# An adaLN model on one core: the steps of both attentions written out instead of looped

## The chip, the core and the metric

The kernel runs on one core of a Trainium2 chip. A core has five engines with an instruction stream each: TensorE (PE, with its weight loads shown as PEld), VectorE (DVE), ScalarE (ACT), GpSimd (POOL) and SyncE (SP), which here issues all DMAs. They meet only through semaphores: an instruction waits until a counter has reached a value, and raises one when it is done. The metric is the time of one execution on the device in microseconds.

## What is computed

Two transformer layers over x of 32 batches of 256 tokens with 128 features, each layer with an attention and a feed-forward part, both scaled and shifted per batch by a modulation table that is computed first. 16 heads of 8 features. Cut to what matters for the change:

```python
# layer 0, attention: no softmax
q, k = l2_normalize(x_norm @ w_q), l2_normalize(x_norm @ w_k)          # per head
resonance = 0.5 + 0.5 * tanh((q @ k.T - 0.27) * 15.0)
fused = (resonance * gate_q[:, None] * gate_k[None, :]) @ v            # gates: sigmoids of q.g_q, k.g_k
x = x + gate * (fused @ w_o + b_o)
# layer 0, feed-forward: 32 x 4 expert slots, tokens picked by the largest logit of their group
# layer 1, attention: rope on q and k, softmax
x = x + gate * (softmax(q @ k.T / sqrt(8)) @ v @ Wo + bo)
# layer 1, feed-forward: ternary weights, gelu-like gate
```

## The kernel before, in words

x stays in on-chip memory from the first step to the last. Four stages follow each other: attention 0 (`attention_0`, from about 30 to 400 us), the experts (`experts_0`, written out, to about 630), attention 1 (`attention_1_bounded`, to about 952; a general form, `attention_1`, is compiled too and chosen by a branch at run time, but isn't run with these inputs) and the feed-forward part (`ffn_1`, a loop of its own over 16 tiles).

Both attentions are software pipelines over the 32 batches. One step b holds, on every engine, work of several batches: TensorE computes the scores of batch b in eight chunks (`scores`), the weighted sums of heads (`heads`), the transposes of keys and queries of batch b+1 (`turn_keys`, `turn_queries`), the projections of b+2 and the transposes of b+3 (`turn`). ScalarE takes each score chunk through tanh (line 686) or exp (line 2439). VectorE normalises, splits q and k into two halves of 16 bits (`a_stack`), copies transposed keys and queries out of PSUM (`a_kT` line 841, `a_qT` line 846), runs a nine-step Newton iteration in attention 0 (`newton_step`, `a_norm2c` first), and adds the residual. GpSimd computes reciprocal roots (`a_rstd`, line 407), applies the modulation and doubles the queries. SyncE loads x and table rows some steps ahead.

The order on each engine is the order in which its `step(b, p)` calls these functions; p is the parity of b and picks one of two buffers. Engines wait with constants where b is a number and with a register's value where b is a loop variable. `stepped` decides which: it writes out the steps up to `pair_first`, then runs a loop of two steps a pass, then writes out the rest. Called as (-3, 33, 4, 12) for attention 0 and (-1, 33, 4, 12) for attention 1, it puts steps 4 to 27 into twelve passes; 0 to 3 and 28 to 31 are written out. In a looped step the address of a tile (`bass.ds(b * TT, TT)`) and the value of a wait (`b * CHUNKS + c`) are computed by register instructions of the engine's sequencer; they appear in the trace as ALU_OP and FUSED_REGOPS, and at the end of a pass there is a COMPARE_BRANCH (line 79). In layer 0 a step of VectorE begins, by the trace, with the copy `a_stack` of line 810, the last instruction of the step before; it is used below as the mark of the step.

Of the kernel before, what the change touches and what calls it, by code (L numbers as in the profile page):

```python
# [24 lines left out]
B = 32  # L25
# [35 lines left out]
def wait(eng, sem, n):  # L61

    if isinstance(n, int) and n <= 0:
        return
    eng.wait_ge(sem, n)
# [9 lines left out]
def stepped(eng, first, last, pair_first, pair_count, step):  # L75

    for b in range(first, pair_first):
        step(b, b % 2)
    with eng.Fori(0, pair_count) as i:
        step(i * 2 + pair_first, pair_first % 2)  # L80
        step(i * 2 + (pair_first + 1), (pair_first + 1) % 2)
    for b in range(pair_first + 2 * pair_count, last + 1):
        step(b, b % 2)
# [210 lines left out]
def attention_0(nc, ctx, dram, sbuf, psum, following):  # L294
# [75 lines left out]
    def rows_of(b, row, n):  # L370
        src = dram["table"]
        src = src[bass.ds(b, 1), row:row + n, :] if not isinstance(b, int) else src[b:b + 1, row:row + n, :]
        return src.rearrange("o r d -> (o r d)").partition_broadcast(P)
# [5 lines left out]
    def there(b):  # L379
        return not isinstance(b, int) or 0 <= b < B  # L380
# [2 lines left out]
        return min(n, B) if isinstance(n, int) else n  # L383

    def every(eng, step):
        stepped(eng, -3, B + 1, 4, 12, step)

    def load(sp, n, p):

        wait(sp, h_done, n - 1)  # L390
        wait(sp, mod_norm_loaded, n * 16)
        sp.dma_start(mod_norm[p][:, :, :], rows_of(n, ROW_CA0, 2)).then_inc(mod_norm_loaded, 16)

        if isinstance(n, int) and n < FIRST:
            return
        wait(sp, x_loaded, (n - FIRST) * 16)
        sp.dma_start(tiles(n), x_rows(n)).then_inc(x_loaded, 16)
# [90 lines left out]
    def run():  # L488
        with nc.Block() as block:
            @block.sync  # L490
            def _(sp):
                def load_gate(n, p):

                    wait(sp, x_biased, n - 1)
                    wait(sp, wo_done, n - 1)
                    sp.dma_start(mod_gate[p][:, :, :], rows_of(n, ROW_GA0, 2)).then_inc(mod_gate_loaded[p], 16)

                def step(b, p):
                    if there(b + 4):
                        load(sp, b + 4, p)  # L500
                    if there(b + 1):
                        load_gate(b + 1, 1 - p)

                load(sp, 1, 1)
                sp.wait_ge(dram["table_stored"], 32)
                load_gate(0, 0)
                load(sp, 2, 0)
                load(sp, 3, 1)

                for dst, src in dram["experts_loads"]:  # L510
                    sp.dma_start(dst, src).then_inc(dram["experts_loaded"], 16)
                for n in range(HB):
                    following["load"](sp, n)
                stepped(sp, 0, B - 1, 4, 12, step)

            @block.tensor
            def _(pe):
# [101 lines left out]
                def step(b, p):  # L619
                    if isinstance(b, int) and b == -2:  # L620
                        pe.wait_ge(wg_done, 2)
                    for pair in range(CHUNKS // 2):
# [23 lines left out]
                        if pair == 3:  # L646
                            if there(b - 1):
                                project_out(b - 1, 1 - p)
                            if there(b + 3) and not (isinstance(b, int) and b == -1):
                                turn(b + 3)  # L650

                every(pe, step)

            @block.scalar
            def _(act):
# [34 lines left out]
                def step(b, p):  # L690
                    for c in range(CHUNKS):
# [6 lines left out]
                        if c == 5 and there(b):  # L698
                            gT_out(b)

                every(act, step)

            @block.gpsimd
            def _(pool):
# [32 lines left out]
                nc.gpsimd.memset(ones16[:, :], 1.0).then_inc(ones_set, 1)  # L737
                pool.wait_ge(ones_set, 1)
                every(pool, step)

            @block.vector
# [1476 lines left out]
def attention_1_bounded(nc, ctx, dram, sbuf, psum, ffn_opening, opening):  # L2218
# [51 lines left out]
    def gate_rows(b):  # L2270
        src = dram["table"]
        src = (src[bass.ds(b, 1), ROW_GA1:ROW_GA1 + 2, :] if not isinstance(b, int)
               else src[b:b + 1, ROW_GA1:ROW_GA1 + 2, :])
        return src.rearrange("o r d -> (o r d)").partition_broadcast(P)

    def there(b):
        return not isinstance(b, int) or 0 <= b < B

    def every(eng, step):
        stepped(eng, -1, B + 1, 4, 12, step)  # L2280


    def sync(sp):
        def load_gate(n, p):

            wait(sp, x_biased, n - 1)
            wait(sp, wo_done, n - 1)
            sp.dma_start(mod_gate[p][:, :, :], gate_rows(n)).then_inc(mod_gate_loaded[p], 16)

        def step(b, p):  # L2290
            if there(b + 1):
                load_gate(b + 1, 1 - p)

        load_gate(0, 0)

        for dst, src in dram["ffn_loads"]:
            sp.dma_start(dst, src).then_inc(dram["ffn_loaded"], 16)
        stepped(sp, 0, B - 1, 4, 12, step)

    def tensor(pe):  # L2300
        def project_v(n, p):
# [79 lines left out]
        def step(b, p):  # L2381
            for pair in range(CHUNKS // 2):
# [24 lines left out]
                if pair == 3:  # L2407
# [9 lines left out]
                    elif b == B - 1:  # L2417
                        ffn_opening["turn"](pe, 1)

        every(pe, step)  # L2420

    def scalar(act):
# [30 lines left out]
    def gpsimd(pool):  # L2453
# [33 lines left out]

        padding(0)
        every(pool, step)

    def vector(dve):
# [98 lines left out]
        every(dve, step)  # L2590

    return {"sync": sync, "tensor": tensor, "scalar": scalar, "gpsimd": gpsimd, "vector": vector}


# [640 lines left out]
```

## Time and profile before

| | us |
|---|---|
| median of 3 runs | 1316.62 |
| lowest, highest | 1313.14, 1316.94 |
| span of the profiled execution | 1317.2 |

The profile is of one execution of the same program, with the start and end of every instruction on every engine. "Idle before" is the time in which an engine did nothing ahead of an instruction, and what follows the arrow is what ended it; "issue" means that nothing the profile shows was waited for. The instructions of a sequencer (waits, register operations, branches) don't count as busy. Half of the span belongs to stages that the change doesn't touch.

### The profile page before, as it was taken

The page shows a single profiled execution, that of the slowest core. Times are in us where ns is not written, and L with a number is a line of the kernel's source. Part 1 is how long each engine was busy: PE and PEld are TensorE (multiplying, and loading weights), DVE is VectorE, ACT ScalarE, POOL GpSimd, SP SyncE. Part 2 cuts the span into 40 slices and gives each one's busy share as a digit, 9 for nine tenths or more (in the row PEclk, how much of TensorE's full clock was granted, in tenths as well). Part 3 has the DMA queues.
Part 4 walks back from the last instruction along what each step waited for, and adds up shares of the span by engine and source line. Part 5 has one row for each costly group of instructions (what it writes and reads, how often), then busy time and mean ns, then how long its engine had stood idle before and what let it go on. Part 6 is the DMA issues. An engine that isn't in the chain of part 4 may idle for free.

```text
span 1317.2 us, 39867 instructions
## 1 busy us (share of the span) xinstructions
PE 1220.9 (93%) x13717; PEld 812.8 (62%) x13717; DVE 1054.6 (80%) x2935; ACT 932.2 (71%) x1338; POOL 574.3 (44%) x793
## 2 busy tenths in 40 slices
PE   3899999999997899987899999999879999999998
PEld 2555555555544666766555555555458877878776
DVE  5799999999976787756899999999646777777763
ACT  0698888888894565542688888888747676766665
POOL 2454444454431243323333343343236565655653
PEclk7799999999999999998899999999979999999999
DMA  5411111111001222100300000000000000000000
GB/s 140 143 33 33 34 36 36 36 36 36 28 10 47 53 50 62 48 19 2 105 14 16 12 12 16 12 12 17 6 2 9 9 16 8 16 8 16 16 8 25
DMA packets 47964, 40.67 MB, mean 31 GB/s; under 512 B 5376, under 2 KB 46688, under 8 KB 47360
## 3 DMA queue, kind: packets, MB, share of 16 engines
q1 hardware_dynamic: 47872, 39.45, 10.6%
q8 instruction: 57, 0.93, 0.3%
q14 instruction: 35, 0.29, 0.1%
HBM read 35.09 MB, written 4.34 MB: 30 GB/s over the span
## 4 chain that ended last, share of the span: by engine, by line
PE 48%; DVE 2%; issue 1%; ACT 0%; POOL 0%; ACTq 0%; DVEq 0%; POOLq 0%
PE psum_all L2821 24%; PE psum_all L2352 9%; PE psum_all L2338 4%; PE psum_all L2121 2%; PE psum_all L2378 1%; PE psum_all L2315 1%; PE psum_all L2324 1%; PE psum_all L2364 1%; PE psum_all L2305 1%; PE psum_all L2370 1%; PE psum_all L2868 1%; PE psum_all L2679 0%; PE psum_all L2113 0%; DVE ffn_gated L2977 0%; DVE ffn_xhat L2670 0%
## 5 line engine op out<-in xcount | busy, mean ns | idle before, releaser
L2439 ACT ACTIVATE a_probs<-psum_all 128x1024 f32<-128x1024 f32 x256 | 248.2, 1022 | 69.2 <-PE psum_all L2338 69.2
L686 ACT ACTIVATE probs<-psum_all,biases 128x1024 f32<-128x1024 f32 x256 | 272.3, 1112 | 34.9 <-PE psum_all L592 34.0
L2821 PE MATMUL psum_all<-ffn_hi,weights_r 128*128 128x512 f32 x704 | 283.8, 403 | 9.4 <-issue 3.8
L2821 PE MATMUL psum_all<-ffn_lo,weights_r 128*128 128x512 f32 x704 | 277.6, 394 | 0.0
L2781 POOL TENSOR_TENSOR ffn_lo<-ffn_full,ffn_hi 128x512 fp32r<-128x512 f32 x143 | 186.7, 1313 | 134.0 <-ACT ffn_hi L2898 97.5
L2821 PEld LDWEIGHTS psum_all<-ffn_hi,weights_r 128*128 128x128 f32 x704 | 133.6, 190 | 50.8 <-DVE ffn_full L2982 9.7
L2821 PEld LDWEIGHTS psum_all<-ffn_lo,weights_r 128*128 128x128 f32 x704 | 134.0, 190 | 25.8
L605 PE MATMUL psum_all<-probs,vpad 128*32 128x257 f32 x2048 | 139.1, 389 | 0.3 <-ACT probs L686 0.3
L2352 PE MATMUL psum_all<-a_probs,vpad 128*32 128x256 f32 x2048 | 137.5, 386 | 0.2 <-DVE a_sums L2517 0.2
L2910 ACT ACTIVATE ffn_full<-psum_all,scales 128x512 f32<-128x512 f32 x128 | 88.3, 690 | 68.5 <-PE psum_all L2821 68.4
L2781 DVE TENSOR_TENSOR ffn_lo<-ffn_full,ffn_hi 128x512 fp32r<-128x512 f32 x64 | 55.2, 862 | 80.3 <-ACT ffn_hi L2913 80.3
L716 POOL TENSOR_TENSOR a_stack<-a_stack,a_ones 128x512 f16<-128x512 f16 x32 | 36.6, 1145 | 123.3 <-DVE a_stack L805 123.3
L2913 ACT ACTIVATE ffn_hi<-psum_all,scales 128x512 fp32r<-128x512 f32 x128 | 87.4, 683 | 0.0
L592 PE MATMUL psum_all<-a_qT,a_kT 32*128 32x256 f16 x1024 | 76.1, 276 | 11.7 <-ACT probs L686 7.8
L605 PEld LDWEIGHTS psum_all<-probs,vpad 128*32 128x32 f32 x2048 | 53.8, 109 | 50.8 <-issue 22.0
L2128 POOL TENSOR_TENSOR a_vareps<-a_moments,eps 128x2 f32<-128x2 f32 x32 | 6.2, 195 | 181.0 <-DVE a_moments L2155 181.0
L2352 PEld LDWEIGHTS psum_all<-a_probs,vpad 128*32 128x32 f32 x2048 | 53.6, 109 | 49.8 <-issue 27.2
L2898 ACT CAST ffn_hi<-ffn_full 128x512 fp32r<-128x512 f32 x64 | 39.7, 620 | 38.1 <-DVE ffn_full L2982 38.1
L2338 PE MATMUL psum_all<-a_qT,a_kT 32*128 32x256 f16 x1024 | 64.7, 274 | 1.8 <-DVE a_qT L2512 1.0
L592 PEld LDWEIGHTS psum_all<-a_qT,a_kT 32*128 32x128 f16 x1024 | 22.9, 92 | 48.0 <-ACT probs L686 35.2
L2904 ACT ACTIVATE ffn_tanh<-psum_all,scales 128x512 f32<-128x512 f32 x64 | 43.5, 687 | 9.4 <-PE psum_all L2821 8.7
L2982 DVE SCALAR_TENSOR_TENSOR ffn_full<-psum_all,scales,ffn_gated 128x512 f32<-128x512 f32 x64 | 48.1, 751 | 2.3
(232 smaller groups left out, 2654.0 us busy)
## 6 DMA issues: line engine op xcount, KB each, us to landing
a_mod_gate<-modulation_table SPq DMA_DIRECT2D x64, 128.0 KB, 2.9
X<-in_x SPq DMA_DIRECT2D x32, 128.0 KB, 2.8
a_mod_norm<-modulation_table SPq DMA_DIRECT2D x32, 128.0 KB, 3.0
f<-in_f SPq DMA_DIRECT2D x2, 2048.0 KB, 10.1
e_mod_norm<-modulation_table SPq DMA_DIRECT2D x32, 128.0 KB, 3.1
out<-X SPq DMA_DIRECT2D x16, 256.0 KB, 2.3
e_gates<-modulation_table SPq DMA_DIRECT2D x32, 64.0 KB, 2.8
weights<-in_h SPq DMA_DIRECT2D x2, 1024.0 KB, 7.7
```

The lines of the kernel that those rows point to most:

```text
L592: last = nc.tensor.matmul(SC[c % 2][:, (TT * r + kb) * T:(TT * r + kb + 1) * T], kT[p][rows, g, kb * P:(kb + 1) * P], qT[p][rows, g, :], s ...
L605: last = nc.tensor.matmul(PO[32 * r:32 * r + 32, :], vpad[p][:, kb, G * r + g, :], probs[:, (2 * g + r // 2) % 4, r % 2, kb, 0:UNIT], star ...
L686: nc.scalar.activation(probs[:, c % 4, :, :, 0:T].rearrange("p r k q -> p (r k) q"), SC[c % 2].rearrange("p (a q) -> p a q", q=T), ACT.Tan ...
L2338: last = nc.tensor.matmul(SC[c % 2][:, (TT * r + kb) * T:(TT * r + kb + 1) * T], kT[p][rows, g, kb * P:(kb + 1) * P], qT[p][rows, g, :], s ...
L2352: last = nc.tensor.matmul(PO[32 * r:32 * r + 32, s * T:(s + 1) * T], vpad[p][:, kb, G * r + g, :], probs[:, (2 * g + r // 2) % 4, r % 2, k ...
L2439: nc.scalar.activation(probs[:, c % 4, :, :, :].rearrange("p r k q -> p (r k q)"), SC[c % 2], ACT.Exp, scale=float(np.float32(1.0) / np.sq ...
L2781: subtract(lo[layer][:, k, :], full[layer][:, k, :], hi[layer][:, k, :].bitcast(F32), ALU.subtract).then_inc(done[layer], 1)
L2821: ins = nc.tensor.matmul(dst, weights[:, w0:w0 + P], part[layer][:, k, :], start=first and i == 0, stop=last and i == len(parts) - 1)
L2904: nc.scalar.activation(tanh[:, m % 2, :], pair(m)[0], ACT.Tanh, scale=scales[:, 0, m:m + 1]).then_inc(tanh_done, 1)
L2910: nc.scalar.activation(full[layer + 1][:, m, :], bank[m % 2], ACT.Gelu, scale=scales[:, 1 + layer, m:m + 1]).then_inc(full_done[layer + 1], 1)
L2913: nc.scalar.activation(hi[layer + 1][:, m, :], bank[m % 2], ACT.Gelu, scale=scales[:, 1 + layer, m:m + 1]).then_inc(hi_done[layer + 1], 1)
L2982: nc.vector.scalar_tensor_tensor(out=full[1][:, m, :], in0=pair(m)[1], scalar=scales[:, 1, m:m + 1], in1=gated[:, m % 2, :], op0=ALU.mult, ...
```

## The change

`every`, through which TensorE, ScalarE, GpSimd and VectorE run their steps, and the calls in the two `sync` functions no longer use `stepped`; all steps are written out, with b a number. Order, parity, work and waits of each step stay what they were; the wait values and addresses become constants. `attention_1` (general) and `ffn_1` keep their loops. The diff:

```diff
@@ -383,7 +383,8 @@
         return min(n, B) if isinstance(n, int) else n
 
     def every(eng, step):
-        stepped(eng, -3, B + 1, 4, 12, step)
+        for b in range(-3, B + 2):
+            step(b, b % 2)
 
     def load(sp, n, p):
 
@@ -511,7 +512,8 @@
                     sp.dma_start(dst, src).then_inc(dram["experts_loaded"], 16)
                 for n in range(HB):
                     following["load"](sp, n)
-                stepped(sp, 0, B - 1, 4, 12, step)
+                for b in range(B):
+                    step(b, b % 2)
 
             @block.tensor
             def _(pe):
@@ -2277,7 +2279,8 @@
         return not isinstance(b, int) or 0 <= b < B
 
     def every(eng, step):
-        stepped(eng, -1, B + 1, 4, 12, step)
+        for b in range(-1, B + 2):
+            step(b, b % 2)
 
 
     def sync(sp):
@@ -2295,7 +2298,8 @@
 
         for dst, src in dram["ffn_loads"]:
             sp.dma_start(dst, src).then_inc(dram["ffn_loaded"], 16)
-        stepped(sp, 0, B - 1, 4, 12, step)
+        for b in range(B):
+            step(b, b % 2)
 
     def tensor(pe):
         def project_v(n, p):
```

## Rows read from the trace of the kernel before

**Rows 1.** The page, busy time, share of the span and instructions of each engine.

```profile
PE 1220.9 (93%) x13717; PEld 812.8 (62%) x13717; DVE 1054.6 (80%) x2935; ACT 932.2 (71%) x1338; POOL 574.3 (44%) x793
```

**Rows 2.** Stretches: length, busy us (instructions) of PE, PEld, DVE, ACT, POOL, clock, DMA, GB/s.

```profile
68.95:79.80 10.85, 10.58 (x135) 6.10 (x134) 10.26 (x38) 10.04 (x15) 5.59 (x9) 1.00 0.14 40
79.80:91.07 11.27, 10.58 (x136) 6.17 (x135) 10.47 (x38) 9.85 (x14) 5.59 (x9) 1.00 0.12 38
91.07:361.57 270.50, 256.87 (x3217) 146.50 (x3216) 252.50 (x888) 241.37 (x314) 134.36 (x216) 1.00 0.12 34
361.57:372.50 10.93, 10.58 (x135) 6.11 (x134) 10.34 (x38) 9.93 (x15) 5.61 (x9) 1.00 0.05 14
685.10:912.00 226.90, 226.90 (x3040) 132.52 (x3039) 218.36 (x530) 184.35 (x208) 83.81 (x138) 1.00 0.05 13
912.00:921.70 9.70, 9.70 (x136) 5.68 (x134) 9.25 (x24) 7.97 (x9) 3.64 (x6) 1.00 0.05 16
```

**Rows 3.** Waits of VectorE in 91.07:361.57 and 685.1:912.0: total us, times, longest.

```profile
DVE a_xhat L446 <- POOL a_rstd L407: 7.7, 24, 0.3
DVE a_stats L429 <- issue: 5.2, 12, 0.5
...
DVE a_hT L2172 <- PE psum_all L2113: 4.4, 12, 0.4
```

**Rows 4.** Timeline of VectorE, loop of attention 0: start us, us, engine, line, operation.

```profile
237.76 0.29 DVE L810 COPY a_stack<-a_stack 128x512 f16<-128x512 f16 x1
...
248.82 0.29 DVE L810 COPY a_stack<-a_stack 128x512 f16<-128x512 f16 x1
249.56 0.49 DVE L429 BATCH_NORM_STATS2 a_stats<-X 128x6 f32 x2 [0.45 <-issue]
...
260.31 0.29 DVE L810 COPY a_stack<-a_stack 128x512 f16<-128x512 f16 x1
```

**Rows 5.** Timeline of VectorE, batch 2 written out, then the looped step from 237.76.

```profile
71.34 0.60 DVE L446 TENSOR_SCALAR a_xhat<-X,a_moments,a_rstd 128x128 f32<-128x128 f32 x2 [0.38 <-POOL a_rstd L407]
...
72.58 0.22 DVE L759 TENSOR_SCALAR a_norm2c<-a_norm 128x64 f32<-128x64 f32 x1
72.72 0.68 DVE L841 COPY a_kT<-psum_all 128x1024 f16<-128x1024 f16 x1
...
240.20 0.60 DVE L446 TENSOR_SCALAR a_xhat<-X,a_moments,a_rstd 128x128 f32 x2 [0.32 <-POOL a_rstd L407]
...
241.43 0.38 DVE L759 TENSOR_SCALAR a_norm2c<-a_norm 128x64 f32<-128x64 f32 x1
241.73 0.68 DVE L841 COPY a_kT<-psum_all 128x1024 f16<-128x1024 f16 x1
```

**Rows 6.** DMA queues (packets, MB, share): whole run, 120:360, 68.95:79.80, 79.80:91.07, 912:921.8.

```profile
q8 instruction: 57, 0.93, 0.3%
q14 instruction: 35, 0.29, 0.1%
...
q1 hardware_dynamic: 11904, 8.39, 12.6%
...
q8 instruction: 2, 0.03, 1.2%
...
q14 instruction: 2, 0.02, 0.6%
...
q8 instruction: 1, 0.02, 0.6%
```

**Rows 7.** Timeline of VectorE, batch 3 written out, and the loop's second step.

```profile
83.86 0.69 DVE L841 COPY a_kT<-psum_all 128x1024 f16<-128x1024 f16 x1 [0.20 <-PE psum_all L592]
...
104.73 0.74 DVE L446 TENSOR_SCALAR a_xhat<-X,a_moments,a_rstd 128x128 f32 x2 [0.32 <-POOL a_rstd L407]
```

**Rows 8.** Timeline of TensorE, fourth pair of scores, a looped step of attention 1 and batch 28.

```profile
800.52 0.70 PE L2338 MATMUL psum_all<-a_qT,a_kT 32*128 32x256 f16 x8
...
918.89 0.62 PE L2338 MATMUL psum_all<-a_qT,a_kT 32*128 32x256 f16 x8
```

## Prediction, written before the result was known

> **What bounds the kernel now.** I read the page first. No engine is idle for long: TensorE is busy for 93% of the span and VectorE for 80% [rows 1]. That mean hides two stages with different limits, so the next view was the table of stretches, cut at the steps of the two attentions [rows 2]. A step is one batch; steps 4 to 27 of each attention run in the loop of two, the others are written out already. This is what makes the case readable: the changed form stands in the trace of before, next to the old one, with the same work.
>
> Attention 0: the 24 looped steps take 270.50 us, 11.27 us each. Written-out steps with the full work are batch 2 (10.85), batch 3 (11.27) and batch 28 (10.93) [rows 2]. Batch 1 has no residual of an older batch, and from 29 on there is less to prepare, so these are no measure. VectorE sets this pace: in 270.50 us it is busy for 252.50, and the waits view has only two entries for it, 7.7 us for the reciprocal root from GpSimd and 5.2 us of "issue", 12 times [rows 2, 3]. TensorE is busy too, but it waits inside the step, for ScalarE and before its transposes.
>
> Attention 1: the looped steps run at 226.90 / 23 = 9.87 us and TensorE shows no idle time at all in 226.90 us; VectorE is busy for 218.36 of them and waits 4.4 us for TensorE [rows 2, 3]. So TensorE (with ScalarE's exponentials, for which it holds the later scores back) sets the pace, and VectorE has a slack of about (226.90 - 218.36) / 23 = 0.37 us a step.
>
> **Attention 0, part by part.** What goes away is sequencer work: a count or address held in a register has to be computed ahead of each wait or access, and the loop's end has an addition, a compare and a branch. Most of it is done while the engine still works on earlier instructions. I looked for the places where it isn't, by laying a looped step of VectorE over a written-out one.
>
> (a) The branch. The step that follows the branch starts with `a_stats` 0.74 us after the last copy of the step before (248.82 to 249.56), with 0.45 us idle, cause "issue"; the other looped step has no such gap [rows 4].  The step without the branch lasts 248.82 - 237.76 = 11.06, the one with it 260.31 - 248.82 = 11.49 [rows 4], a difference of 0.43. Twelve pairs: 12 x 0.43 = 5.2 us.
>
> (b) The registers. The step without the branch is still 11.06 - 10.85 = 0.21 us longer than batch 2. The place is one: from `a_norm2c` to the copy of the keys, 72.58 to 72.72 written out (0.14) against 241.43 to 241.73 in the loop (0.30), with `a_norm2c` drawn out from 0.22 to 0.38 us [rows 5]. That is 0.16 of it; before it, another 0.1 us is paid at the head of the step and mostly given back, since `a_xhat` waits for GpSimd anyway (0.38 us written out, 0.32 in the loop) [rows 5]. 24 x 0.21 = 5.0 us.
>
> Together 10.2 us, or by the table 24 x (11.27 - 10.85) = 10.1 us, if every step ran like batch 2.
>
> (c) What is added: instructions that have to be fetched. The loop bodies stay where they are: between 120 and 360 us all packets (11904) are of the data queue, and no instruction is loaded [rows 6]. The whole run has 57 packets of 16 KB on TensorE's instruction queue (q8) and 35 of 8 KB on the one of the others (q14) [rows 6]. Written-out steps load some each: batch 2 of attention 0 has two of q8, batch 3 two of q14, batch 28 of attention 1 one of q8 [rows 6], and with the other queue's it is two or three. 44 further steps are written out (22 in each attention, since a body of two was there), so about 44 x 2 = 88 more packets, 1 MB, nothing for the DMA engines, which are 12 to 14% busy. The question is whether the engine stands still for a fetch. Batch 3 says that it can: VectorE has 0.20 us idle before the copy of the keys, put down to a matmul that was long done [rows 7], and further on a `newton` step is drawn out; the step is 0.42 longer than batch 2, and a packet of q14 starts in it. In the loop, which is entered at 91, the last packet of q14 starts at about 105.8, and there `a_xhat` takes 0.74 instead of 0.60 [rows 5, 7], 0.14 lost. So 0.14 to 0.42 us for a block on VectorE, and not in every step. The trace of before doesn't show 24 such steps in a row; bounds are 0 (all like batch 2) and 0.42 a step (all like batch 3, the gain is nil). I take the mean of the three full steps, (10.85 + 11.27 + 10.93) / 3 = 11.02, since these contain blocks of every engine in about their natural number. Then attention 0 gains 24 x (11.27 - 11.02) = 6.0 us.
>
> The Trainium skill, Runtime: NRT & Kernel Launch, section Instruction fetch mechanics, says that an engine fetches its next block by itself while it runs the current one and that crossing a block costs one tail bump, mostly hidden. By that rule the sum for attention 0 would be 10.1 us and not 6.0; batch 3 is the row that speaks against it. The skill's Advanced Engine Details and Errata, section Control Flow Timing, prices a compare-and-branch at about 108 ns; by that (a) would be 12 x 0.11 = 1.3 us. The 0.45 us row decides against it.
>
> **Attention 1.** Same edits, other limit. Branch and registers of VectorE, ScalarE, GpSimd lie beside TensorE's work. On TensorE one row moves: the fourth pair of scores takes 0.70 us in the loop (held by the exponentials) and 0.62 in batch 28, written out [rows 8]; 226.90 us over 23 steps is 9.87 each, so 9.79 would be left. 24 x 0.08 = 1.9 us. Batches 1 to 3 of this attention don't serve: ScalarE also rounds the weights there. Fetches on VectorE are worth up to 0.42 us but fall on a slack of 0.37 a step; fetches on TensorE cost nothing in batch 28, which had one [rows 6]. Bounds: 0 and, if the same 0.08 came off once more, 3.8. I take 1.9.
>
> **The rest.** The work of SyncE (loads three steps ahead) has slack in both forms. Steps 0 to 3 and 28 to 31, the experts and the feed-forward part don't change; blocks fall elsewhere in them, worth some tenths either way. The clock is at its full level (1.00) in every stretch of rows 2, so there is nothing to win or lose by it there. Sum: 6.0 + 1.9 = 7.9 us. The profiled execution took 1317.2, so 1309.3; it lay 0.6 above the median of the runs (1316.62), so **1308.7 us** for the median.
>
> **The rivals.**
> 1. *The fetch is hidden* (batch 3 was an accident). 10.1 + 1.9 = 12.0 us: 1316.6 - 12.0 = 1304.6. For it: batches 2 and 28 with 2 or 3 packets each are near the shortest steps. Against it: batch 3, and the 0.14 in the loop's second step. Chance 0.22. (It is also what the rule of the Trainium skill named above would give.)
> 2. *The gain goes into a new wait.* When VectorE gets faster, the next thing late is TensorE's transposes and the key path between the two engines, or the blocks of VectorE cost 0.42 in most steps, as in batch 3. Then attention 0 stays at about 11.2 and attention 1 gives 0 to 1.9: 1314 to 1316.6, say 1315. For it: TensorE has nearly no idle time in batch 2 (10.58 of 10.85 busy) [rows 2]. Chance 0.18.
> 3. *Slower: blocks stall every engine on the path.* 88 packets more, TensorE's among them, at 0.42 us each are 37 us, less the 12 that loop and registers give back: 1316.6 + 25 = 1342. It decides from 12 / 88 = 0.14 us a block. For it: the price 0.42 is seen once. Against: batch 2 has two packets of TensorE's queue and is the shortest full step, and batch 28 of attention 1 has one of each queue and beats every looped one. Chance 0.05.
> 4. *The forecast*, 1308.7; chance 0.55. Its own range is 1306 to 1312.
>
> That the change doesn't do what it says can be left out: the written-out form is the one of steps 0 to 3.
>
> **How the numbers follow.** Range: from rival 1 and a little of the 3.8 bound, 1303, to rival 2 near no change, 1315.5; beyond it lie rival 3 and the outer part of rival 2. One measurement of this kernel can tell about 0.3%, 3.9 us, from no change. Faster by more than that: all of rival 1, nearly all of the forecast, 0.22 + 0.54; with a small part of rival 2 it is 0.77. Within: 0.18. Slower: 0.05.
>
> **What would show it.** In the profile after: no register or branch rows on the two attentions; instruction packets at 100 or more on q8 and about 60 or more on q14, spread over all 40 slices of the attentions; VectorE's step of attention 0 at 10.85 in most batches, with single steps of about 11.2 where a block comes; the copy of the keys 0.14 behind `a_norm2c`; attention 1 at 9.79 with the fourth pair of scores at 0.62. The prediction is wrong if a step of attention 0 has idle time put down to "issue" on TensorE or ScalarE (blocks there count too), or if attention 1 runs above 9.87.

## The result and the profile after

The changed kernel took 1299.58 us (median of 4 runs, 1298.88 to 1303.03), beside 1314.88 for the kernel before on the same chip: ratio 0.9875, 95% interval 0.9847 to 0.9904, so faster by 1.25%, clear of noise. It is 17.0 us below the median of 1316.62 in the table of before, where 7.9 were forecast, and lies under the range, which ended at 1303.0.

How much of this is the kernel? The mean granted clock differs from run to run (0.962 to 0.978 for the kernel before, 0.968 to 0.976 for the changed one). All ten runs of the changed kernel, with those of e12 below, have a median of 1302.0, against 1315.6 for 83 runs of the kernel before that were taken beside the experiments. At a like clock the means differ by 12.8 us (0.972: 1303.2 in 3 runs against 1316.0 in 10) and 12.1 us (0.976: 1299.6 in 2 against 1311.7 in 7). So about 13 us belong to the kernel; the first four runs lay at the lucky end.

The profiled execution has a span of 1301.1 us, against 1317.2. Its page, busy time and the DMA queues (columns as in [rows 1] and [rows 6]):

```profile
PE 1212.8 (93%) x13717; PEld 808.6 (62%) x13717; DVE 1047.7 (81%) x2935; ACT 929.9 (71%) x1338; POOL 575.0 (44%) x793
...
q8 instruction: 104, 1.70, 0.5%
q14 instruction: 64, 0.52, 0.1%
```

Counts of work are those of [rows 1], and instruction packets went from 57 and 35 to 104 and 64. The table of stretches, cut at VectorE's steps as in [rows 2] (batch 2, batch 3, batches 4 to 27, batch 28), then 24 steps of attention 1, cut at TensorE's first scores (batches 5 to 28):

```profile
67.73:78.59 10.86, 10.63 (x136) 6.16 (x135) 10.26 (x37) 10.05 (x15) 5.59 (x9) 1.00 0.13 38
78.59:89.87 11.28, 10.58 (x136) 6.17 (x135) 10.48 (x38) 9.93 (x15) 5.60 (x9) 1.00 0.18 39
89.87:351.06 261.19, 253.99 (x3217) 146.35 (x3216) 246.66 (x889) 238.44 (x314) 134.47 (x216) 1.00 0.13 37
351.06:361.92 10.86, 10.59 (x135) 6.11 (x134) 10.26 (x37) 9.93 (x15) 5.60 (x9) 1.00 0.05 14
668.73:903.63 234.90, 234.90 (x3169) 138.29 (x3168) 225.82 (x552) 192.34 (x216) 87.60 (x144) 1.00 0.06 16
```

The 24 steps of attention 0 went from 270.50 to 261.19 us, 10.88 each: nearly batch 2's 10.86, and not the forecast's 11.02. In attention 1 a step takes 234.90 / 24 = 9.79 us, as forecast. The queues in 89.87:351.06 show that the blocks do come there, where [rows 6] had none:

```profile
q1 hardware_dynamic: 13024, 9.18, 12.5%
q8 instruction: 26, 0.43, 0.7%
q14 instruction: 19, 0.16, 0.2%
```

VectorE's waits in the 24 steps of attention 0, to be laid beside [rows 3]: the 12 gaps of "issue" are gone, and the wait for GpSimd has grown from 7.7 to 9.3 us, as written-out steps have it (0.38 and not 0.32 in [rows 5]).

```profile
DVE a_xhat L447 <- POOL a_rstd L408: 9.3, 24, 0.4
DVE a_rnorm L784 <- DVE a_newton L780: 0.2, 1, 0.2
```

The prediction named idle time of "issue" on TensorE in a step of attention 0 as a sign of being wrong. By the letter it is there, but small, and the steps follow VectorE all the same:

```profile
PE psum_all L528 <- issue: 0.5, 2, 0.3
```

The timeline of VectorE in one of these steps, for [rows 4] and [rows 5] (line numbers are 1 or 2 higher; 231.32 to 242.19 is the step, 10.87 us; the copy of the keys starts 0.15 behind `a_norm2c`, which takes 0.23):

```profile
231.32 0.29 DVE L812 COPY a_stack<-a_stack 128x512 f16<-128x512 f16 x1
231.53 0.48 DVE L430 BATCH_NORM_STATS2 a_stats<-X 128x6 f32<-128x128 f32 x2
...
233.72 0.60 DVE L447 TENSOR_SCALAR a_xhat<-X,a_moments,a_rstd 128x128 f32<-128x128 f32 x2 [0.39 <-POOL a_rstd L408]
...
234.95 0.23 DVE L761 TENSOR_SCALAR a_norm2c<-a_norm 128x64 f32<-128x64 f32 x1
235.10 0.68 DVE L843 COPY a_kT<-psum_all 128x1024 f16<-128x1024 f16 x1
...
242.19 0.29 DVE L812 COPY a_stack<-a_stack 128x512 f16<-128x512 f16 x1
```

And TensorE's fourth pair of scores, [rows 8]:

```profile
725.04 0.62 PE L2342 MATMUL psum_all<-a_qT,a_kT 32*128 32x256 f16 x8
```

Where the time went, by stage, in every kernel that was profiled. Stages are cut at VectorE's last copy of a step (attention 0), at the start of the last weighted sum of heads (end of "tail"), at TensorE's first scores of a step (attention 1) and at the first matmul of the feed-forward (all in us, from the times of the trace; "half" is the time in the experts for which the granted clock stood at 1.2 instead of 2.4 GHz):

```
kernel                    head  att.0 4-27  tail  experts (half)   head 1  att.1 4-27  tail 1  feed-fwd   span
before                   91.07    270.51   38.72  230.37 (20.5)    43.94    236.92    48.61    357.10   1317.2
before, e13              90.72    270.45   38.70  226.17 ( 6.8)    43.94    236.93    48.77    356.75   1312.4
after                    89.87    261.19   38.68  225.09 (10.2)    43.94    235.07    49.18    358.03   1301.1
after, e12               90.83    261.05   38.67  226.12 (17.1)    43.93    235.07    49.16    358.25   1303.1
e1  attention 0 only     89.93    261.05   38.66  226.11 (10.2)    43.95    236.93    49.72    357.12   1303.5
e2  attention 1 only     90.11    270.42   38.71  227.45 (10.2)    43.94    235.05    48.68    356.78   1311.1
e3  VectorE only         91.47    263.59   38.65  230.67 (23.9)    43.93    236.96    48.43    356.99   1310.7
e8  VectorE and GpSimd   90.01    262.48   38.69  226.89 (13.7)    43.94    236.93    48.33    357.35   1304.6
e4  four steps a pass    89.64    267.63   38.70  231.81 (10.1)    44.69    236.95    48.51    357.93   1315.8
e7  VectorE +64          90.69    260.82   38.67  224.87 (10.2)    43.94    235.07    48.52    356.94   1299.5
e5  TensorE +64         94.06    261.16   38.68  231.16 ( 9.8)    43.81    235.09    48.91    357.34   1310.2
e6  TensorE +128       105.88    261.15   38.68  222.30 (10.2)    44.06    235.09    48.98    356.78   1312.9
e10 TensorE +64 spread   90.65    261.16   39.09  232.76 (16.8)    43.74    235.06    49.04    357.05   1308.5
e9  TensorE +128 spread  90.19    265.23   39.82  226.94 (13.7)    44.10    235.05    49.07    356.73   1307.1
e11 feed-forward too     90.25    261.25   38.66  228.43 (10.2)    43.94    235.08    49.50    353.83   1301.0
e14 the same again       90.91    261.19   38.67  222.63 ( 6.8)    43.94    235.06    49.26    355.69   1297.3
```

Two columns are steady to some 0.2 us among kernels of the same form, and carry the change: attention 0 gives 9.3 us and attention 1 gives 1.85, 11.2 together. The third part of the difference is in the experts, where no instruction was changed.

### The profile page after: what moved, and what is told of

Same layout as the page of the kernel before. It is cut to its first block, busy times and chain, and to the rows that moved or that the text cites. A ratio compares the mean times of both kernels' runs of the same rounds, so it can differ in the third digit from the quotient of the medians.

```text
span 1301.1 us, 37745 instructions
## 1 busy us (share of the span) xinstructions
PE 1212.8 (93%) x13717; PEld 808.6 (62%) x13717; DVE 1047.7 (81%) x2935; ACT 929.9 (71%) x1338; POOL 575.0 (44%) x793
## 4 chain that ended last, share of the span: by engine, by line
PE 48%; DVE 3%; issue 1%; ACT 0%; POOL 0%; ACTq 0%; DVEq 0%; POOLq 0%
PE psum_all L2825 25%; PE psum_all L2356 9%; PE psum_all L2342 4%; PE psum_all L2123 2%; PE psum_all L2382 1%; PE psum_all L2319 1%; PE psum_all L2328 1%; PE psum_all L2368 1%; PE psum_all L2309 1%; PE psum_all L2872 1%; PE psum_all L2374 1%; PE psum_all L2683 1%; PE psum_all L2115 0%; DVE ffn_gated L2981 0%; DVE ffn_xhat L2674 0%
## 5 line engine op out<-in xcount | busy, mean ns | idle before, releaser
L594 PE MATMUL psum_all<-a_qT,a_kT 32*128 32x256 f16 x1024 | 74.2, 275 | 9.4 <-ACT probs L688 8.1
L2342 PE MATMUL psum_all<-a_qT,a_kT 32*128 32x256 f16 x1024 | 63.0, 274 | 1.8 <-DVE a_qT L2516 1.0
L2981 DVE SCALAR_TENSOR_TENSOR ffn_gated<-ffn_tanh,psum_all 128x512 f32<-128x512 f32 x64 | 43.6, 681 | 8.5 <-ACT ffn_tanh L2908 8.5
## 6 DMA issues: line engine op xcount, KB each, us to landing
f<-in_f SPq DMA_DIRECT2D x2, 2048.0 KB, 10.2
```

The source lines that it names most:

```text
L594: last = nc.tensor.matmul(SC[c % 2][:, (TT * r + kb) * T:(TT * r + kb + 1) * T], kT[p][rows, g, kb * P:(kb + 1) * P], qT[p][rows, g, :], s ...
L2342: last = nc.tensor.matmul(SC[c % 2][:, (TT * r + kb) * T:(TT * r + kb + 1) * T], kT[p][rows, g, kb * P:(kb + 1) * P], qT[p][rows, g, :], s ...
```

## The experiments

The theory behind the record was: branch and registers cost 10.1 us in attention 0, and fetched blocks give back 4.1. Its rival 1 said that the blocks are hidden. After the result a second question came up: why a stage that the change doesn't touch moves by 5 us.

**One attention at a time.** e1 writes out the steps of attention 0 alone, e2 those of attention 1 alone:

```diff
-        stepped(eng, -3, B + 1, 4, 12, step)
+        for b in range(-3, B + 2):
+            step(b, b % 2)
```

> Attention 0 written out, attention 1 as before. Theory S (the gain lies in the steps): the 24 formerly looped steps of attention 0 run at 10.85 to 10.9 us but for two or three with a stall, 9.3 us less than before; attention 1 keeps 9.87 a step. Time 9 to 10 us under before, and whatever is more than that comes from stretches at half clock in the experts part, so it varies from run to run with the granted clock. Rival E (the rest of the 16 us belongs to how attention 0 hands over to the experts): 14 us or more under before in every run, at whatever clock.

> Attention 1 written out, attention 0 as before. Theory S: attention 0 at 11.27 on average, attention 1 at 9.79 a step, fourth pair of scores 0.62 us; 1.9 us under before, plus or minus what the clock does. Rival E: the same 1.9. Rival that attention 1 carries the unexplained 5 us: 6 us or more under before.

e1: 1303.07 us, ratio 0.9905 (0.9878 to 0.9933), 12.3 us under the median beside it: more than the 9 to 10 that the steps were to give, less than rival E's 14. e2: 1313.24 us, ratio 0.9988 (0.9968 to 1.0007), which can't be told from no change in time, while its trace shows the 1.9 us in attention 1. The parts add up: 9.5 us in attention 0 with e1, 1.9 in attention 1 with e2, each absent in the other.

**Which engine's loop costs.** e3 writes out VectorE's steps of attention 0 and leaves the other engines in their loops; e8 does so for VectorE and GpSimd.

```diff
-                every(dve, step)
+                for b in range(-3, B + 2):
+                    step(b, b % 2)
```

> Only VectorE's steps of attention 0 are written out; the other four engines and all of attention 1 keep their loops. If VectorE's own sequencer work sets the pace: steps of 10.9 to 10.95, 8 to 9 us of the 9.3. If the register work of GpSimd, ScalarE or TensorE lies on the path too: steps of 11.0 or more, alternating with their branches, and 4 to 6 us.

> VectorE's and GpSimd's steps of attention 0 written out, the other three engines looped. VectorE alone gave steps of 10.96 on average, 0.08 over the written-out 10.88. If GpSimd's registers ahead of the reciprocal root (for which VectorE waits) are the rest: 10.88 a step and the full 9.3 us in attention 0. If TensorE's or ScalarE's are: 10.96 again.

e3: 1309.79 us, ratio 0.9951 (0.9925 to 0.9976); the 24 steps take 263.59 us, 6.9 of the 9.3 us gained. e8: 1306.74, ratio 0.9929 (0.9903 to 0.9955); 262.48 us, 8.0 of 9.3. Both lie between the two cases that were named for them: steps of 10.98 us for e3 and 10.94 for e8. What is left after e8 is 1.3 us and stands in every other step (stretches of e8, two steps in a row; the second is batch 15, which is 0.08 long in the kernel after too):

```profile
199.39:210.39 11.00, 10.78 (x136) 6.22 (x135) 10.44 (x38) 10.24 (x14) 5.59 (x9) 1.00 0.12 36
210.39:221.31 10.92, 10.43 (x135) 6.04 (x135) 10.38 (x37) 9.86 (x13) 5.59 (x9) 1.00 0.20 37
```

Most of the others alternate between 10.99 and 10.87. Taken off in this order, VectorE's own loop was 6.9 us, GpSimd's, which prepares the reciprocal root for which `a_xhat` waits, 1.1, and those of TensorE, ScalarE and the loads 1.3; which of these three carries the 1.3 was not tried. The longer steps in e3 say that VectorE's gap was not the whole price: the others' loops show, with 0.1 us a step, once VectorE's is gone. With all of them written out that goes too. Rival 2 expected a new wait of some 0.4 us a step, and the kernel after has none: the wait for GpSimd grew by 0.07 a step, and most steps are as short as batch 2.

**The branch alone.** e4 keeps both loops, with four steps a pass and six passes:

```diff
+    body = 4 if pair_first == 4 else 2
-    with eng.Fori(0, pair_count) as i:
-        step(i * 2 + pair_first, pair_first % 2)
-        step(i * 2 + (pair_first + 1), (pair_first + 1) % 2)
+    with eng.Fori(0, 2 * pair_count // body) as i:
+        for j in range(body):
+            step(i * body + (pair_first + j), (pair_first + j) % 2)
```

> Both attentions stay loops, with four steps a pass and six passes instead of two steps and twelve. If the branch costs 0.43 us on VectorE wherever it falls and the registers 0.21 in every step: three steps of 11.06 and one of 11.49 a pass, 11.17 on average, 2.6 us less in attention 0 and nothing in attention 1. If the branch stall grows with the length of the body (the target has to be fetched anew): packets of the instruction queues in the loop and more than 0.43 behind each branch, and no gain.

Attention 0: 267.63 us, 2.9 less; the waits of VectorE in the six passes show half of the twelve gaps of [rows 3]:

```profile
DVE a_xhat L447 <- POOL a_rstd L408: 7.5, 24, 0.3
DVE a_stats L430 <- issue: 2.5, 6, 0.5
```

Steps are three of 11.04 and one of 11.48, so a branch is 0.44 us and registers are 11.04 - 10.87 = 0.17 a step: term (a) as forecast and term (b) a little less than its 0.21 (with the 11.06 of the kernel before it is 0.19). But the kernel took 1318.01 us, ratio 1.0036 (1.0008 to 1.0064), no faster than before and, if anything, 0.4% slower: the experts need 231.8 us, at the same 10 us of half clock with which e2 needs 227.5. This was the first sign that the experts depend on code that runs ahead of them.

**A block of VectorE.** Batch 3 takes 11.28 us in the kernel after, too, with 0.20 us idle before the copy of the keys, as in [rows 7] (put down to "issue" here), and `a_seed` drawn out. The drawn-out `newton` step of the prediction is no sign of it: from batch 3 on one of them takes 0.56 to 0.60 us in every step, here an earlier one than usual.

```profile
82.22 0.23 DVE L761 TENSOR_SCALAR a_norm2c<-a_norm 128x64 f32<-128x64 f32 x1
82.65 0.69 DVE L843 COPY a_kT<-psum_all 128x1024 f16<-128x1024 f16 x1 [0.20 <-issue]
83.26 0.42 DVE L765 TENSOR_SCALAR a_seed<-a_norm2c 128x64 int32<-128x64 int32 x1
```

e7 puts 64 writes of one column each on VectorE before its first step, which moves every later instruction by at least 64 places in VectorE's code:

```diff
+                for i in range(64):
+                    nc.vector.memset(spare[:, i:i + 1], 0.0)
                 every(dve, step)
```

> The written-out kernel with 64 tiny memsets more at the head of VectorE's attention 0 program. In every kernel so far batch 3 lasts 11.28 us, in the written-out ones batch 5 11.03, 15 10.94 and 22 11.09, all others 10.86. If these are blocks of VectorE's instructions, the long steps move by about one batch (64 of some 56 instructions a step), so 11.28 at batch 2 or 4 and 10.86 at batch 3. If they belong to the work of batch 3 (a load of x, a table row), 11.28 stays at batch 3.

1301.13 us, ratio 0.9894 (0.9848 to 0.9939). Batch 3 (79.83:90.69) now takes 10.86 us, and the same place reads:

```profile
83.46 0.23 DVE L762 TENSOR_SCALAR a_norm2c<-a_norm 128x64 f32<-128x64 f32 x1
83.61 0.68 DVE L844 COPY a_kT<-psum_all 128x1024 f16<-128x1024 f16 x1
84.21 0.28 DVE L766 TENSOR_SCALAR a_seed<-a_norm2c 128x64 int32<-128x64 int32 x1
```

The gap belongs to the place of VectorE's code, then, and not to the work. It did not just move on by a batch, as was expected: no step of 11.28 is left. What a block costs depends on where in the step it falls: of the 27 steps from batch 2 on, after has four long ones (batches 3, 5, 15, 22: +0.42, +0.17, +0.08, +0.23 over 10.86), e7 has two of 10.93. All others are at 10.85 to 10.88, with 19 packets of the other engines' queue in the 24 steps of after. The trace also shows that VectorE doesn't wait for the packet seen there: its gaps in batches 3, 5 and 22 of after end at 82.65, 108.28 and 286.08, and the packets start at 83.32, 108.94 and 286.74, 0.66 to 0.67 us behind. That it stands still at the step into a block already there, and asks for the next one after that, would fit, but is not shown.

**TensorE's blocks in the experts.** e5 and e6 add 32 and 64 small matmuls (64 and 128 TensorE instructions) at the end of the setup, e10 and e9 add as many, spread over the 32 steps of attention 0; they compute again what stands there.

```diff
 # e5, e6 (range(64)), behind the setup's last matmul
+            for _ in range(32):
+                nc.tensor.matmul(psum[:, 3584:3584 + B], wmod[:, 1, 0:D], cond_silu[:, 1, :], start=True, stop=True)
 # e10, e9 (range(2)), in project_out of attention 0
                     for t in range(TT):
+                        if t == 1:
+                            for _ in range(1):
+                                nc.tensor.matmul(PP[:, 0:32], oT[:, 0:P], wo_gated[p][:, 0:32], start=True, stop=True)
```

> The written-out kernel with 32 small matmuls more at the end of TensorE's setup program (64 instructions, into a bank nobody reads then), so that every later block of TensorE's instructions begins 64 instructions earlier in the work. Theory B (part of the unexplained time in the experts is TensorE standing still for a block of instructions): the idle time of TensorE put down to issue moves to other matmuls of the experts, and the experts part changes by 1 to 6 us in either direction from the 225 us of the profile after, at like half-clock time. Rival C (only the clock varies it): the issue gaps stay before the same matmuls and the experts part follows the time at half clock alone. Attention steps unchanged in both.

> The same with 64 small matmuls (128 instructions). Theory B: other places again for the issue gaps in the experts, a third duration. Rival C: same places as before the shift.

> The same with 64 TensorE instructions more (one such matmul a step). Place of the blocks: experts 230 to 232 us as in e5, with idle time of TensorE put down to issue of 12 to 14 us there, attention 0 unchanged, so 1304 to 1308 us. If e5's long experts came from its changed head: 224 to 227 and 1298 to 1303. Nothing of the computation is changed.

> The kernel after, with 128 TensorE instructions more ahead of the experts, as in e6, but spread over the 32 steps of attention 0 (two matmuls of 32 columns, with their loads, beside the output projection of each step; they write again what stands there), where VectorE sets the length of a step. Nothing of the computation is changed. If the length of TensorE's code ahead of the experts decides where TensorE stands still in them (theory 'place of the blocks'): experts 222 to 223.5 us as in e6, steps of attention 0 still 10.85 to 10.9, and the head at 90 and not 106, since no work is added to it: 1296.5 to 1299.5 us. If e6's short experts came from what the clock did after its changed head instead: experts at 225 or above, and 1299 to 1303.

e5: 1313.86 us, ratio 0.9987 (0.9963 to 1.0011). e6: 1316.49, ratio 1.0026 (1.0006 to 1.0046). e10: 1311.28, ratio 0.9951 (0.9932 to 0.997). e9: 1309.15, ratio 0.9936 (0.9914 to 0.9958). Shifted by 64, the experts take 231.2 and 232.8 us; shifted by 128, 222.3 and 226.9. The waits of TensorE in the experts say why (the rows for "issue"; first after, then e10; e5 has 8.0 us in 5 as well):

```profile
PE psum_all L1197 <- issue: 1.6, 2, 1.0
PE psum_all L1248 <- issue: 0.3, 1, 0.3
```

```profile
PE psum_all L1200 <- issue: 8.1, 5, 2.1
PE psum_all L1251 <- issue: 0.3, 1, 0.3
```

One place of e10 in the timeline of TensorE, and the queue of TensorE's code in 575:583:

```profile
575.36 1.61 PE L1200 MATMUL psum_all<-e_slots,f 128*32 128x64 f32 x99
578.50 2.25 PE L1200 MATMUL psum_all<-e_slots,f 128*32 128x64 f32 x127 [1.53 <-issue]
582.80 0.94 PE L1200 MATMUL psum_all<-e_slots,f 128*32 128x64 f32 x30 [2.05 <-issue]
```

```profile
q8 instruction: 2, 0.03, 1.8%
```

Between the two stalls lie 127 matmuls with their weight loads, some 254 instructions, and they are done in 2.25 us. The two packets start at 575.86 and 580.20 and take 1.19 and 1.15 us; TensorE goes on at 578.50 and 582.80, 1.5 us behind the end of each. So the second block came 4.30 us after the first, which had lasted 2.25. At 9 ns an instruction a block is used up sooner than the next one is ready; in the attentions, where 135 matmuls with their loads fill 10.9 us (some 40 ns an instruction), it isn't, and the steps don't show it. The link between stalls and packets holds in all 16 profiles: leaving out the matmuls of L1246 (L1248 and L1251 in other kernels), whose gaps keep no fixed distance from a packet, TensorE stands for "issue" for more than 0.2 us 51 times in the experts, and each time it goes on 1.2 to 1.8 us after a packet has ended. At a like 9.8 to 10.2 us of half clock eight kernels needed 222.3 to 231.8 us; less these stalls, 220.9 to 224.4. The Trainium skill, Runtime: NRT & Kernel Launch, section Instruction fetch mechanics, has blocks of 16 KiB, 256 instructions; the trace agrees on TensorE (16384 bytes a packet on that queue, 254 instructions between stalls), while the packets of the other engines' queue have 8192 bytes. Its "mostly hidden" holds for the attentions and fails here, at up to 2.1 us a block.

Some of it went another way than thought. e6's head grew by 16 us, with half clock for 51.2 us instead of 37.5: its 64 small matmuls stand between the setup and the attention and take some 0.2 us each there (102 matmuls in 20.2 us). e9's steps went to 11.05 us instead of 10.9, though VectorE was thought to hide four small instructions a step. Its waits have a new row, which is nearly the whole 4.0 us by which the 24 steps grew: VectorE now waits for TensorE's transposes, the wait that rival 2 had in mind.

```profile
DVE a_hT L752 <- PE psum_all L528: 3.9, 21, 0.2
```

And e9's experts took 226.9, not 222 to 223.5, and e10 has 8.4 us of "issue" and not 12 to 14. The shift by 128 did not move the stalls to other places, as was expected of e6: after has them 89 and 184 us behind the start of the experts, e6 87 and 182, e9 89 and 185 (e5 and e10 both have them near 94, 140, 146, 187 and 192). So the shift by 128 is as good as none, and no better; why it comes back after 128 is not shown. That e6 had 222.3 at the half clock of after, and 0.2 us less of stalls, is not explained by either and lies in the spread between executions, of which more now.

**The same kernels once more.** e12 is the kernel after, e13 the kernel before, both unchanged.

> The kernel after, unchanged, once more. If the 5.3 us that the experts are shorter belong to the kernel: experts at 225 to 227 us again, with 10.2 us of half clock or near it, 1298 to 1302 us and a ratio of 0.986 to 0.990. If most of it belonged to that execution: experts at 228 to 231, and 1301 to 1306.

> The kernel before, unchanged, once more. If the experts' length belongs to the kernel: 229 to 231 us again with idle time of TensorE put down to issue of 8.9 us, 1.7 to 2.0 us of it 142 to 145 us behind their start. If to the execution: 225 to 228. Time 1313 to 1318 us, ratio 1.

e12: 1303.07 us, ratio 0.9884 (0.9846 to 0.9922). e13: 1317.13, ratio 1.0 (0.9966 to 1.0035). Taken one by one they point both ways: e12's experts at 226.1 us are where they were expected if the shorter experts belong to the kernel, e13's at 226.2 where they were expected if they belong to the execution. The experts as stretches of before, e13, after and e12, then their "issue" rows over 0.4 us in before, e13 and e12 (for after they stand above):

```profile
400.29:630.66 230.37, 198.82 (x3696) 149.84 (x3688) 165.84 (x499) 109.73 (x243) 73.44 (x130) 0.96 0.18 46
```

```profile
399.87:626.03 226.16, 194.51 (x3695) 144.20 (x3688) 165.78 (x499) 109.72 (x243) 73.53 (x130) 0.98 0.18 47
```

```profile
389.74:614.83 225.09, 195.52 (x3695) 145.41 (x3688) 165.69 (x499) 109.93 (x243) 73.55 (x130) 0.98 0.18 46
```

```profile
390.54:616.66 226.12, 196.62 (x3695) 146.91 (x3688) 165.32 (x499) 109.92 (x243) 73.41 (x130) 0.96 0.18 46
```

```profile
PE psum_all L1152 <- issue: 1.7, 1, 1.7
PE psum_all L1195 <- issue: 1.0, 1, 1.0
PE psum_all L1246 <- issue: 0.9, 2, 0.7
PE psum_all L1222 <- issue: 0.8, 1, 0.8
```

```profile
PE psum_all L1152 <- issue: 1.5, 1, 1.5
PE psum_all L1195 <- issue: 1.3, 1, 1.3
PE psum_all L1222 <- issue: 0.7, 2, 0.5
```

```profile
PE psum_all L1197 <- issue: 1.5, 2, 1.2
PE psum_all L1248 <- issue: 0.9, 2, 0.7
```

The same kernel before differs from itself by 4.2 us in the experts, with a granted clock of 0.96 in one execution and 0.98 in the other. TensorE's busy time differs by 4.3 us and its idle time by 0.1: the matmuls were longer, as the clock has it, and the waits were not. So a good part of the 5.3 us between the first two profiles was the clock. The two kernels before have 13.7 us of half clock in the mean, and so have the two after; their means are 228.3 and 225.6 us, 2.7 apart. The stall of 1.5 to 1.7 us at L1152 and the one of 0.5 to 0.8 at L1222 are in both profiles of before and in none of after, 2.0 to 2.5 us. Against that, the stalls at L1195, L1197 in after, are some 0.4 longer there; the net is 3.4 us of block stalls before and 1.6 after, 1.8 of the 2.7. (The 0.7 at L1246 is no block's: in before it comes 7.4 us behind the start of a packet, and in e13 and after the same gap stands as a wait for `e_delta`.) It is not the luck of two profiles: e2, e3 and e8 run the same code of TensorE as before up to the experts' end and have the stall at L1152 (1.4 to 2.0 us), and e1, e7, e11 and e14 run that of after and haven't.

**A version that goes further.** e11 and e14 are the same kernel: the one after, with the feed-forward's loop written out as well.

```diff
-        step(0)
-        step(1)
-        with eng.Fori(2, NT - 2) as n:
+        for n in range(NT):
             step(n)
-        step(NT - 2)
-        step(NT - 1)
```

> The kernel after, with the last feed-forward's loop over row tiles written out as well, on every engine. There TensorE sets the pace and its loop has one step a pass. If what a loop costs is the branch and the registers on the engine that sets the pace, and TensorE's is near nothing because its instructions run from a queue ahead of the array: the feed-forward stays at 357 to 358 us, the whole at 1298 to 1302. If TensorE stands still at blocks there as it does in the experts: 1 us for each block of 16 KB, with some 14 tiles more written out, 2 to 8 us longer. If a branch costs TensorE what it cost VectorE (0.4 us a pass): some 5 us shorter.

> The kernel after with the feed-forward's loop written out too, once more. In e11 its feed-forward took 353.8 us against 358.0 (after) and 357.1 (before), with 12.5 us of half clock against 16.7 and 12.4. If the loop costs TensorE something: 353 to 355 us again, and in time 2 to 4 us less than e12 beside it. If that was the clock of one execution: 356 to 358, and the two within 1 us of each other.

e11: 1300.01 us, ratio 0.9862 (0.9821 to 0.9904). e14: 1300.02, ratio 0.9877 (0.9837 to 0.9916). The feed-forward got shorter, and by less than the 5 us of a branch at VectorE's price. Their ten runs have a median of 1300.0 us, against 1302.0 for ten of after; side by side on one chip it was 1300.02 (e14) against 1303.07 (e12). The intervals overlap, so the time alone doesn't prove it, but the trace shows it: two row tiles in the middle of the feed-forward take, in e12 and then in e14,

```profile
1071.90:1114.70 42.80, 42.80 (x194) 34.19 (x194) 31.91 (x63) 29.64 (x48) 26.02 (x23) 1.00 0.04 12
```

```profile
1068.00:1110.20 42.20, 42.20 (x194) 34.44 (x193) 31.71 (x63) 29.67 (x48) 25.70 (x23) 1.00 0.05 13
1110.20:1152.60 42.40, 42.40 (x194) 34.59 (x193) 31.84 (x63) 29.73 (x49) 25.91 (x23) 1.00 0.05 13
```

with TensorE busy throughout as the profile models it: 0.4 to 0.6 us for two tiles, 2.2 to 3.5 us over the stage at a like amount of half clock (353.8 against 356.8 to 357.4 with 12.0 to 12.6 us; 355.7, with 17.8, against 357.9 to 358.3 with 16.6 to 16.9). All 16 profiles settle it: from the second tile's first matmul to the last tile's, at full clock throughout, a tile takes 21.32 to 21.34 us in the mean in each of the 14 with the loop, and 21.13 in both without. A loop costs an engine that is busy all the time something too, 0.2 us a tile. Which of its waits, or which other engine's loop, carries that was not tried.

e11 and e14 also show what stays open. They are one kernel, and their experts took 228.4 and 222.6 us. A stall of 2.2 us at L1197, 46 us behind the start, is in e11 (and, with 2.4 us, in e1) and not in e14, e7, after or e12, which run the same code of TensorE up to there, and 3.4 us of half clock are worth about 1.0 (before against e13: 4.2 us for 13.7); some 2.5 us remain unexplained. A block's stall may come in one execution of a kernel and not in another, then, and one profile settles a stage like this to no better than some 3 us.

## Why the prediction was wrong where it was

**The bound.** Right. VectorE set the pace in attention 0, TensorE in attention 1; the gains are 9.3 and 1.85 us on the same 24 steps each.

**Terms (a) and (b), branch and registers.** Right, (b) a little large. The sum of 10.1 us counts on every step like batch 2; the 24 steps came to 10.88 instead of 10.85, and e4 put the branch at 0.44 and the registers at 0.17 us a step by themselves (0.43 and 0.21 in the prediction). One detail was wrong: the difference was read as VectorE's alone. e3 shows that 2.4 us of it belong to the loops of the other engines, which lay under VectorE's.

**Term (c), the blocks, is the step that failed.** It took 0.17 us a step, the mean of three written-out steps of which one was an outlier, "since these contain blocks of every engine in about their natural number". They did, but the number is not what costs: the place is. It gave back 4.1 us. Measured: 9.3 gained of 10.1, so 0.8 us given back in 24 steps, 0.03 a step. The three long steps among them carry 0.48; the rest is that an ordinary step takes 10.86 to 10.87 and not 10.85. With 3 steps as a sample, one of them 0.42 long, the mean was set by that one. Nor were the 0.08 of batch 28 a block's: it takes 10.89 to 10.93 behind a loop of VectorE (before, e13, e2, e4) and 10.84 to 10.87 where VectorE has none, but for e9 with its longer steps. As for batch 3, e7 shows that without a block at that place it is a step of 10.86 as well. The prediction had this case as rival 1, at 0.22, and its 12.0 us for both attentions compare with 11.2.

**Attention 1.** Right: 1.85 for 1.9, and the fourth pair of scores at 0.62. No step had time for a stall: TensorE's busy time equals the stretch.

**"Blocks fall elsewhere in them, worth some tenths either way".** The second step that failed, mis-sized by a factor of up to ten, and this is what the prediction had least ground for: the trace of before had it in the experts, 29 packets of TensorE's code in 230 us and stalls of 1.7, 1.0 and 0.8 us put down to "issue". Against the kernel before, the place of the code is worth about -2 us in the kernel after and, by the same mechanism, +5 in e10 or e4 (stalls of 1.6, 8.1 and 8.3 us against 3.4).

**The clock.** "Nothing to win or lose there" was said of the stretches of rows 2 and holds for them. The experts were not among them, and there the same kernel differed by 4.2 us between two executions. The single profile of before, with a span of 1317.2 us, was a high one; its repeat had 1312.4. The prediction put it 0.6 above the median of the runs, but a span is 1.7 to 2.2 us shorter than the time of the same execution in all later runs (after: 1301.1 and 1303.03), so it lay some 2.6 above, an estimate. The forecast doesn't hang on it, since 1316.62 - 7.9 gives it directly.

**The sum.** Measured: 9.3 + 1.85 + some 2 in the experts, about 13, and 12 to 13 at a like clock. Forecast: 7.9. Of the 5 us missing, 3.3 are term (c), 2 the experts. The remaining 3.4 between 17.0 and the 13.6 of all runs are the draw: the 3 of before lie 1.0 above the median of 83, the 4 of after 2.4 below that of all ten, 1302.0, which itself is under the range's low end by 1.0. With rival 1's full 12.0 and the experts' 2, the range would have begun at 1302.6. The prediction took its single mean as the likely case, although its own rows for the short steps were those of rival 1.

**Rival 3** (blocks stall everything, from 0.14 us a block): 47 more packets of TensorE's and 29 more of the others' cost at most 0.8 us in attention 0 and nothing that shows in attention 1, 0.01 us each (the prediction had counted on 88). Its mechanism is real, though, in a place it wasn't looked for: five stalls of TensorE in e10.

## What to carry to other kernels

Where an engine sets the pace of a short loop, its branch and registers are on the path: here 0.44 us a pass and 0.17 a step, and the loops of the other engines add 0.1 us a step behind it. Writing the steps out paid that back nearly whole where instructions were long (some 40 ns each on TensorE), and no block was late there; ask for the place of the blocks where many short instructions follow each other (9 ns each in the experts). An edit that changes the length of an engine's code can move the stalls in all that follows (1.4 to 8.3 us of them in the experts of this kernel), so a small gain is to be judged by the stage it is in and not by the total alone.

## What the runs showed of the hardware that was not expected

- TensorE can use up a 16 KB block in 2.25 us (127 matmuls of 64 columns with their loads) and then stands for 1.5 to 2.1 us (e10). It goes on 1.2 to 1.8 us after a packet has ended, in all 51 stalls of the 16 profiles; the packets of e10 took 1.15 and 1.19 us.
- Batch 3 is 0.42 us longer with the place of VectorE's code in the kernel after, and not at all with 64 instructions more ahead of it (e7); 19 packets in 24 steps cost at most 0.8 us in all. VectorE's gaps end 0.66 us before a packet starts.
- 64 more TensorE instructions ahead of the experts made them 5 to 8 us longer (e5, e10), 128 more did not (e6, e9).
- In the experts, half clock for 13.7 us more went with 4.2 us more between two executions of one kernel, and the stall of 2.2 us came in e11 and not in e14, which are the same kernel.
- A tile of the feed-forward, with TensorE without idle time, takes 21.13 us without the loop (e11, e14) and 21.32 to 21.34 with it.
